# Attention in units of four heads, with the key sums on GpSimd and the shift rows sent by a DMA that ScalarE starts

## What is computed

```python
h = _sln(hidden, w, ...)                    # layer norm, scaled and shifted per batch by a condition
qkv = (h @ Wqkv.T + bqkv)                   # 16 heads of 32
energy = einsum('bhqd,bhkd->bhqk', q, k)
att = softmax(energy, axis=-1) / D ** 0.5
out = einsum('bhqk,bhkd->bhqd', att, v) @ Wp.T + bp
h1 = out + hidden
return _sln(h1, w, ...) + h1
```

## Time and profile before

| | |
|---|---|
| median of 3 runs | 1630.13 us (1624.61 to 1631.23) |
| the profiled execution | 1630.67 us, span 1628.9 us |
| TensorE busy | 1490.8 us (92%), mean granted clock 0.964 |
| VectorE / ScalarE / GpSimd busy | 977.9 / 722.8 / 395.5 us |
| DMA | 162.17 MB, mean 100 GB/s |

### The profile page before, as it was taken

One profiled execution on the slowest core, in us unless ns is written; L12 is line 12 of the kernel. 1 busy time (PEld: TensorE's weight loads), 2 busy tenths in 40 slices (PEclk: granted clock), 3 DMA queues, 4 the chain that ended last, 5 costly groups with the idle time before them and its releaser, 6 DMA issues. The chain is left out here.

```text
span 1628.9 us, 21550 instructions
## 1 busy us (share of the span) xinstructions
PE 1490.8 (92%) x7204; PEld 896.1 (55%) x7204; DVE 977.9 (60%) x1454; ACT 722.8 (44%) x1250; POOL 395.5 (24%) x266
## 2 busy tenths in 40 slices
PE   6979899999999628999999999999999999999993
PEld 4636666666666425555655654655654655554632
DVE  2533676667666623556666666666666666666675
ACT  0231342334233242565465465465465465465471
POOL 1013443334332141011042041032042042041032
PEclk9999899999999858999999999999999999999997
DMA  9453233223331243223124124124124124123121
GB/s 301 167 204 79 83 134 140 105 109 139 133 136 53 81 161 104 49 63 118 42 67 141 45 63 136 43 65 144 43 64 143 41 66 141 46 62 107 46 54 66
DMA packets 97176, 162.17 MB, mean 100 GB/s; under 512 B 39104, under 2 KB 47616, under 8 KB 90928
## 3 DMA queue, kind: packets, MB, share of 16 engines
q1 hardware_dynamic: 95920, 160.44, 31.9%
q10 hardware_dynamic: 1152, 0.41, 0.1%
HBM read 72.67 MB, written 37.78 MB: 68 GB/s over the span
## 5 line engine op out<-in xcount | busy, mean ns | idle before, releaser
L1171 DVE TENSOR_REDUCE mx<-a_bank 128x1 f32<-128x512 f32 x512 | 340.0, 687 | 226.0 <-PE a_bank L1356 223.6
L1071 ACT ACTIVATE pt<-a_bank 128x512 f32<-128x512 f32 x512 | 277.2, 595 | 148.8 <-PE a_bank L1381 145.9
L1395 PE MATMUL a_bank<-pt,v 128*32 128x512 f32 x1024 | 272.5, 608 | 0.0
L1397 PE MATMUL a_bank<-pt,ones 128*32 128x512 f32 x1024 | 272.5, 608 | 0.0
L1356 PE MATMUL a_bank<-sk_stack,sq_stack 96*128 96x512 f32 x512 | 207.6, 446 | 5.2 <-DVE mx L1171 2.0
L1356 PEld LDWEIGHTS a_bank<-sk_stack,sq_stack 96*128 96x128 f32 x512 | 88.5, 189 | 187.8 <-DVE mx L1171 135.1
L1381 PE MATMUL a_bank<-sq_stack,sk_stack 98*128 98x512 f32 x512 | 169.6, 408 | 2.8 <-ACT pt L1071 1.4
L742 PE MATMUL g_bank<-m,sf 128*128 128x320 f32 x512 | 155.1, 446 | 1.9 <-issue 1.9
L1062 ACT ACTIVATE sq_stack<-a_bank 2x512 fp32r<-2x512 f32 x128 | 69.0, 583 | 146.9 <-PE a_bank L1365 146.7
L48 PE MATMUL a_bank<-hh,wqkh 128*128 128x512 f32 x256 | 107.2, 419 | 25.4 <-POOL hl L971 24.6
L1381 PEld LDWEIGHTS a_bank<-sq_stack,sk_stack 98*128 98x128 f32 x512 | 96.6, 191 | 43.9 <-ACT pt L1071 15.1
(11 more groups left out here) (166 smaller groups left out, 2652.1 us busy)
## 6 DMA issues: line engine op xcount, KB each, us to landing
sq_stack<-qh SPq DMA_DIRECT2D x256, 64.0 KB, 2.0
sk_stack<-kh SPq DMA_DIRECT2D x256, 64.0 KB, 2.0
m_rows<-mout SPq DMA_DIRECT2D x8, 1280.0 KB, 5.0
m<-m_rows SPq DMA_DIRECT2D x8, 1280.0 KB, 5.7
xraw<-in_x_t SPq DMA_DIRECT2D x8, 1024.0 KB, 7.7
xn<-in_x SPq DMA_DIRECT2D x8, 1024.0 KB, 5.2
h_rows<-xn SPq DMA_DIRECT2D x8, 1024.0 KB, 4.0
t_rows<-hout SPq DMA_DIRECT2D x8, 1024.0 KB, 3.9
```

The lines of the kernel that those rows point to most:

```text
L1071: nc.scalar.activation(pt[:, i, k, :], bank[:, k, :], ACT.Exp).then_inc(s["exp_done"], 1)
L1171: nc.vector.reduce_max(mx[:, p % 2, n, k:k + 1], bank[:, 2 + i % 2, :], AX).then_inc(s["emax_done"], 1)
L1395: nc.tensor.matmul(bank[a:a + DH, 4 + p % 2, :], v[:, bpar, i, (2 * p + k) * DH:(2 * p + k + 1) * DH], w, start=i == 0, stop=i == NT - 1)
L1397: last = nc.tensor.matmul(bank[r:r + DH, 4 + p % 2, :], ones32[:, :], w, start=i == 0, stop=i == NT - 1)
```

## The change

**In the attention stage** the unit is a chunk of four heads, in sixteen slots. A slot is one L1381-like matmul (now L1392), one L1356-like matmul for the chunk after (now L1405), and one `mm3` of a projection. The weighted sums fill the four column groups of the array with four heads (`weighted`, in slots 2 and 14). The denominators come from one group of four matmuls in slot 5 on `acc`, which GpSimd has summed over the four key tiles (`key_sum`: six additions of 128x1024 per chunk). The maxima's parts are transposed by one matmul for two heads, copied by ScalarE to `sht`, and brought to `sq_stack` by a DMA that ScalarE issues. VectorE takes reciprocals (128 columns at a time, slots 6 to 9) and quotients straight from PSUM. The last layer norm works tile by tile.

**In the graph stage** the bias `bp` is added to `xn` by GpSimd (`add_bp`) before `h_rows` is stored, and the split of `hout` into `houth` (ScalarE) and `houtl` (GpSimd, `lo_rows`) is done there, with both stored. The attention stage then loads both parts; ScalarE issues these DMAs and those of `h`.

```diff
@@ graph, sync @@
             def store_h(b, four):
-                sp.wait_ge(s["h_done"], four)
+                sp.wait_ge(s["hb_done"], four)
                 sp.dma_start(d["h_rows"][ds(b, 1)].rearrange("o p t f -> (o p) t f"), xn[:, :, :]).then_inc(s["h_stored"], 16)
...
                 store_h(b - 1, 4 * b)
                 sp.wait_ge(s["h_stored"], 16 * b)
-                sp.wait_ge(s["ln_done"], 4 * b)
                 load_x(b)
@@ graph, gpsimd @@
+            def add_bp(b):
+
+                for i in range(NT):
+                    pool.wait_ge(s["ln_done"], 4 * b + i + 1)
+                    nc.gpsimd.tensor_tensor(xn[:, i, :], xn[:, i, :], bp[:, :], ALU.add).then_inc(s["hb_done"], 1)
+
+            def lo_rows(b):
+
+                for f in range(FC):
+                    pool.wait_ge(s["lnt_done"], 4 * b + f + 1)
+                    nc.gpsimd.tensor_tensor(houtl[:, f, :], hout[:, f, :], houth[:, f, :].bitcast(F32),
+                                            ALU.subtract).then_inc(s["hl_done"], 1)
+
             def step(b, par, last):
                 if not last:
                     front(b + 1)
+                if not (isinstance(b, int) and b == 1):
+                    lo_rows(b - 2)
                 softmax(b, True)
+                add_bp(b - 1)
                 if not last:
                     label_products(b + 1)
@@ graph, scalar @@
                 nc.scalar.activation(hout[:, f, :], bank[:, 2 + f, :], ACT.Identity,
+                                     bias=bcol[:, f, ds(b, 1)], scale=gcol[:, f, ds(b, 1)])
+                nc.scalar.activation(houth[:, f, :], bank[:, 2 + f, :], ACT.Identity,
                                      bias=bcol[:, f, ds(b, 1)], scale=gcol[:, f, ds(b, 1)]).then_inc(s["lnt_done"], 1)
@@ attention, gpsimd @@
+            def key_sum(b, c, half, step):
+                G, two = 4 * b + c, slice(2 * half, 2 * half + 2)
+                done = 6 * G + 3 * half
+                if step == 0:
+                    pool.wait_ge(s["exp_done"], SLOTS * G + 8 * half + 4)
+                    if half == 0 and not start(b, c):
+                        pool.wait_ge(s["den_ready"], G)
+                    nc.gpsimd.tensor_tensor(acc[:, two, :], pt[:, 0, two, :], pt[:, 1, two, :],
+                                            ALU.add).then_inc(s["sum_done"], 1)
+                else:
+                    pool.wait_ge(s["exp_done"], SLOTS * G + 8 * half + 2 * step + 4)
+                    pool.wait_ge(s["sum_done"], done + step)
+                    nc.gpsimd.tensor_tensor(acc[:, two, :], acc[:, two, :], pt[:, step + 1, two, :],
+                                            ALU.add).then_inc(s["sum_done"], 1)
@@ attention, scalar @@
+            def shift_copy(b, c, half):
+                n = 2 * (4 * b + c) + half
+                act.wait_ge(s["sh_ready"], n + 1)
+                if not (isinstance(b, int) and n == 0):
+                    act.wait_ge(s["shrow_in"], 16 * n)
+                nc.scalar.activation(sht[:, :], bank[0:4 * NT, XB, 0:P], ACT.Copy).then_inc(s["sht_done"], 1)
+                act.wait_ge(s["sht_done"], n + 1)
+                act.dma_start(sq[3 * DH:3 * DH + 2, c % 2, 2 * half:2 * half + 2, :].bitcast(F32)
+                              .rearrange("o k (n c) -> o (k n) c", c=P), sht[:, :]).then_inc(s["shrow_in"], 16)
@@ attention, vector @@
+            def batch(b, bpar, more):
+                for c in range(FC):
+                    shift_parts(b, c, 1)
+                    for slot in range(SLOTS):
...
+                        if slot == 5 and (c < 2 or more):
+                            lo_part(*ahead(b, c, 2), 0)
+                        if 6 <= slot < 10 and former:
+                            reciprocals(*former, slot - 6)
+                        if slot == 7 and (c < 3 or more):
+                            shift_parts(*ahead(b, c, 1), 0)
+                        if slot == 9 and (c < 2 or more):
+                            lo_part(*ahead(b, c, 2), 1)
+                        if slot == 10 and former:
+                            quotients(*former)
...
+                        if slot >= 14 and c == 2:
+                            output_lo(b, slot - 14)
@@ attention, tensor @@
+            def weighted(b, vpar, c, part):
...
+                for i in (2 * part, 2 * part + 1):
+                    for j in range(HC):
+                        last = nc.tensor.matmul(bank[DH * j:DH * j + DH, OB, :],
+                                                v[:, vpar, i, (HC * c + j) * DH:(HC * c + j + 1) * DH], pt[:, i, j, :],
+                                                start=i == 0, stop=i == NT - 1)
+                last.then_inc(s["pv_done"], 1)
...
+                    for slot in range(SLOTS):
+                        scores_t(b, c, slot)
+                        if following:
+                            scores(*ahead(b, c, 1), slot)
+                        piece(b, c, slot, more)
+                        if slot == 2:
+                            shift_t(b, c, 1)
+                            if former:
+                                weighted(*former, 1)
+                        if slot == 5 and former:
+                            denominators(former[0], former[2])
+                        if slot == 11 and following:
+                            shift_t(*ahead(b, c, 1), 0)
+                        if slot == 14:
+                            weighted(b, bpar, c, 0)
```

More of the change, by code:

```diff
@@ L888, in first, with start @@
             return isinstance(b, int) and b == 0
+        def start(b, c):
+            return first(b) and c == 0
         def batches(eng, batch):
@@ new lines, in batch @@
+            def batch(b, bpar, more):
+                later = not first(b)
+                for c in range(FC):
+                    if not start(b, c):
+                        key_sum(*(ahead(b, c, -1) if c else (b - 1, 3)), 1, 2)
+                    if later and c in (1, 2):
+                        rsqrt(b - 1, 2 * c - 2)
+                    if later and c in (2, 3):
+                        result(b - 1, 2 * c - 3)
+                    key_sum(b, c, 0, 0)
+                    if later and c in (1, 2):
+                        result(b - 1, 2 * c - 2)
+                    key_sum(b, c, 0, 1)
+                    key_sum(b, c, 0, 2)
+                    key_sum(b, c, 1, 0)
+                    if later and c in (1, 2):
+                        rsqrt(b - 1, 2 * c - 1)
+                    key_sum(b, c, 1, 1)
@@ L1136, in _ @@
+            load_t(0)
+            load_h(0, 0)
+            load_h(0, 1)
+            act.wait_ge(s["ld_c"], 16)
             for k in range(4):
@@ new lines, in piece @@
+            def piece(b, c, slot, more):
+                unit, f = divmod(slot, FC)
+                later = not first(b)
+                here = (c < 2 or more, c < 2 or more, c == 0 or (c < 3 and later) or (c == 3 and more),
+                        (c < 2 and later) or (c >= 2 and more))[unit]
+                if not here:
+                    return
+                if f == 0:
+                    bank_free(b, c, unit, more)
+                if unit < 2:
+                    project(*ahead(b, c, 2), unit, f)
+                elif unit == 2:
+                    if c == 0:
+                        values(b, 3, QB, f)
+                    elif c == 3:
+                        values(b + 1, 1, QB, f)
+                    else:
+                        output(b - 1, 2 * c - 1, QB, f)
```

894 lines of the change are left out of this document (431 added, 463 removed).

## The result

The changed kernel takes 1677.9 us (median of 4 runs, 1675.64 to 1681.43), against 1629.35 us before in the runs taken beside it. The ratio is 1.0304 with a 95% interval of 1.0275 to 1.0334: 3% slower. The forecast was 1674, 2.7% slower. The profiled execution has a span of 1673.8 us, 44.9 longer than the 1628.9 before.

A forecast was written before the change was run, and what follows sets the result against it. TensorE's work was taken to bound both stages. From 1630.7 us, +100 in the graph stage, -46 in the attention loop, -5 between the stages and -6 in the tail gave 1674 us, range 1595 to 1730.

The forecast's parts named there:

- The wait for `xraw`: Graph stage: ScalarE waits 13.0 us for `xraw`, behind bias additions and the store, in five steps, all on TensorE's path.
- 7 + 8 - 5: Last graph step's late labels +7, additions and stores at the stage's end +8, GpSimd's split gone before the attention stage -5.
- The attention loop: All loop terms of the attention stage together: -167 + 45 + 74 + 16 - 14 = -46 us.
- TensorE's work: Attention loop: TensorE's work per chunk of four heads falls from 30.0 to 24.6 us, a gain of 5.4.
- -167 and -14: Attention loop: -167 us for TensorE's lighter chunks over 32 chunks, and -14 by sums over the whole loop.
- The burst: Attention loop, slots 6 to 10: VectorE's 9.0 us of work costs TensorE 1.4 us per chunk, +45 us.
- GpSimd in VectorE's way: Attention loop: VectorE's SBUF instructions wait for the GpSimd addition under way, 1.2 us on average, +74 us.
- 16 for the last two chunks: Attention loop's end: TensorE has little work, GpSimd's 18 to 24 us bound the last two chunks, +16.
- The DMA of the shift rows: Attention loop: ScalarE's two DMAs per chunk are hidden; if not, they would cost 1 us per chunk.
- The tail: Behind the attention loop: the layer norm goes tile by tile, -6 us.
- C: Rival, attention stage: VectorE bounds it, both shift parts wait for an addition; chunks 31 to 32 us, 1750; chance 0.16.
- A: Rival, attention stage: stays bound by TensorE, stalls below 2.0 us per chunk, loop gains 130, total 1575; chance 0.19.

The follow-up runs named there:

- g_order: Changed kernel with the sync engine's store of `h_rows` and load of `xn` one step later, behind the issue of `xraw`; 1639.0 us, ratio 1.0060.
- g_labels: Changed kernel with GpSimd's label products ahead of the bias additions in the graph stage, sync engine's queue as it was; 1691.7 us, ratio 1.0403.
- g_fix: Changed kernel with `xraw` issued ahead of the store, label products ahead of bias additions, and GpSimd's wait for `bp` moved to its first use; 1610.1 us, ratio 0.9894.
- a_small_both: Changed kernel with `key_sum` additions 16 columns wide and each reciprocal 8 columns wide instead of 128, all waits kept; 1582.0 us, ratio 0.9713.
- a_small_sums: Changed kernel with GpSimd's `key_sum` additions 32 elements wide instead of 1024, number, order and waits kept; 1596.0 us, ratio 0.9790.
- a_sync_dma: Changed kernel with the DMA of the shift rows issued by the sync engine instead of by ScalarE; 1679.7 us, ratio 1.0305.
- the quarters: Changed kernel with each `key_sum` addition on GpSimd cut into four of 256 elements, all work kept; 1622.2 us, ratio 0.9950.
- the halves: Changed kernel with each `key_sum` addition on GpSimd cut into two of 512 elements, all work kept; 1651.0 us, ratio 1.0130.
- g_spread: Changed kernel with `xraw` issued ahead of the store, a late wait for `bp`, and bias additions in GpSimd's pauses within the softmax; 1598.7 us, ratio 0.9801.

## Why the prediction was right, and where not

The time (1677.9 for 1674) and the direction came as forecast. By its own steps:

**The wait for `xraw`.** Forecast 13.0 us in five steps; ScalarE's five waits are 12.57, 14.45, 13.25, 12.59 and 13.11, a mean of 13.2. The five steps grew by 349.8 - 264.0 = 85.8 us for 85 forecast. Inside this sum two sizes were off and met: TensorE's idle time grew by 12.5 us a step (from 12.15 to 74.85 in five), where I had 13.0 and 1.5, and its busy time, for the clock, by 4.6 (from 251.85 to 274.95), where I had 2.5. That the store in the queue causes the wait is shown by g_order and g_labels. What I had wrong is its cover: I took the wait to be the only one and the label products as late in the last step alone. A second wait of 5 us lay under the first, and it came out when the first was removed, with the clock lost behind it. The sum didn't need it, the remedy did.

**The first step.** It starts 8.2 us later (128.87 for 120.63), which no term held. GpSimd waits at its start for `bp`, which the sync engine issues at 116.15 us, behind `adj` and `m`:

```profile
123.80 4.92 POOL L481 TENSOR_TENSOR xl<-xraw,xh 128x512 fp32r<-128x512 f32 x4 [8.24 <-DMA bp<-in_bp]
```

The wait stood in the diff, ahead of GpSimd's first instruction, and I read only its place in the steps. g_fix shows it: 121.4.

**The last step to the attention stage.** From the eighth self features to the first matmul of the attention stage it takes 131.8 us (576.29 to 708.11) against 119.6: +12.2 for 7 + 8 - 5 = 10. The -5 is wrong in its sign. GpSimd's split is gone, but TensorE's wait at this place is 27.45 us for 24.60, and it is VectorE's split of the weights that ends it; so 7 + 8 were 9.4.

```profile
708.11 0.80 PE L48 MATMUL a_bank<-hh,wqkh 128*128 128x512 f32 x1 [27.45 <-DVE wqkl L1346]
```

From there to the first scores with keys on partitions it takes 4.7 us more, for which there was no term.

**The attention loop.** From its first such scores to its last it takes 1636.56 - 749.04 = 887.5 us, against 947.1 before: -59.6 for -46. The nearness is partly luck. *TensorE's work:* 24.6 per chunk forecast and 24.24 measured, so this was right; but a loop without burst and sums still takes 799.5 us (a_small_both), 147.6 less than before and not the 181 that -167 and -14 make, since waits for DMAs and ScalarE fill part of what is freed. I had no term for those. *The burst:* this is the term that was mis-sized. 45 forecast, and alone it is worth 14 in the whole time, 9 of them in the loop. VectorE's work in it was summed rightly (9.1 us by the means of a_small_sums, for 9.0), but TensorE waits for maxima 0.5 us per chunk (16.3 us over 31 chunks) and not 1.4, and other small waits take the place of these when the burst is gone. *GpSimd in VectorE's way:* 74 forecast on top of the burst, and 16 for the last two chunks; without the sums the kernel gains 82. The mechanism and the 1.2 us of mean wait (1.36 less 0.17 measured) were right. The rows of before showed less for it than I wrote: only the maxima read PSUM there, its reciprocals and quotients read SBUF (L1188, L1193); that reads from PSUM keep their time is shown by the changed kernel. *The sum:* 45, 74 and 16 make 135, where both together are 887.5 - 799.5 = 88 in the loop (96 in the whole time). Priced each alone they would be 14 and 39, so they can't be priced alone either: VectorE's lead is one and the same slack, and what one delay leaves of it the other uses up. The 33 us too much of gain and the 47 too much of loss cancelled, down to 14.

**What no term held.** 8.2 at the first step, 4.7 at the head of the attention stage and 2.2 between the stages stand against the 14 that the loop did better. That the total came within 4 us is owed to that too.

**The DMA of the shift rows** was taken as hidden. TensorE waits for it 2.3 us in 800, so nearly all of it is, and a_sync_dma shows that its issuer does not matter. **The tail**, from the last of those scores to the end, takes 37.2 us for 42.5: -5.3 for -6.

**The rivals.** C, both shift parts caught, did not come: the second part has a mean of 0.42 us in the changed kernel. It is at 0.68 in the quarters and 1.04 in the halves. There one addition follows another at once, so where the first part ends with the one, the second meets the next. A asked for stalls below 2.0 us per chunk; they are (112.9 - 102.8)/4 = 2.5.

## What to carry to other kernels

Put no instruction that waits long ahead of a load in a queue that issues in order, and ask of every late instruction which others stand behind it: here one group of additions delayed a DMA queue and VectorE's labels at once, and mending one of the two made things worse or half as good. Work given to an idle GpSimd isn't free where VectorE works on SBUF beside it; cut it into short instructions, or spread it over GpSimd's own pauses at a place where TensorE doesn't wait for either, even if it then takes longer in all. Two delays that draw on the same slack must be priced together: each alone looks cheap (14 and 39 us here), and both together cost more than the sum of that (96). And an edit that moves a piece of work to another engine does not test what the piece costs.

## What the runs showed of the hardware

A GpSimd addition in twice as many instructions of half the width costs 8% more of GpSimd's time (2.45 to 2 x 1.32) and makes the kernel 27 us faster; in four, 22% more and 56 us faster. I had expected the shorter ones to lose part of it at their starts.

TensorE idled 2.25 us in g_fix and then ran the next five microseconds at 0.50 of its clock, which is 1.2 GHz; in g_spread the wait at the same place is 0.97 us, and the clock stays at 1.00 in the five behind it:

```profile
411.00:416.00 5.00, 4.42 (x24) 3.11 (x24) 3.01 (x5) 4.44 (x9) 3.41 (x3) 1.00 0.00 0
```

A small wait can thus cost more than its own length.
